# Attention of a two-stage kernel: two PSUM pairs become one ring of four, and GpSimd's and VectorE's work is put in another order

## What is computed

```python
x1 = x + tanh(g_xattn) * cross_attention(layernorm(x), ctx)          # not touched
y = layernorm(x1)
q, k = heads(y @ Wq), heads(y @ Wk)                                  # 8 heads of 64
gl_v = (y @ Ws).reshape(b, t, h, e)                                  # 5 experts
wv = topk_mask(gl_v, 2) * sigmoid(gl_v)
xv = einsum('btd,edk->btek', y, Wv)
v = einsum('bthe,btek->bhtk', wv, xv)                                # values, mixed over experts
probs = softmax(einsum('bhid,bhjd->bhij', q * scale, k))
attn = einsum('bhij,bhjd->bihd', probs, v)
mask_o = topk_mask((y @ Wd).reshape(b, t, h, e), 2)
out = einsum('bthe,bthk,ekd->btd', mask_o, attn, Wo)                 # expert results, summed over heads
return x1 + tanh(g_ffn) * out
```

## Time and profile before

| | |
|---|---|
| median of 3 runs | 1397.97 us (1397.93 to 1398.26) |
| the profiled execution, its time | 1396.65 us |
| its span in the profile | 1394.9 us |
| PE, DVE, ACT, POOL busy over the span | 90%, 63%, 46%, 53% |
| first layer / second layer | to 565 us / from 565 us to the end |

### The profile page before, as it was taken

How to read it: one execution, slowest core, us unless ns; L and a number is a source line. 1 busy time by engine, 2 the same in 40 slices (tenths; PEclk the granted TensorE clock), 3 DMA queues, 4 the chain that set the end, 5 groups by cost and what they waited for, 6 DMA issues and landing times.

```text
span 1394.9 us, 20101 instructions
## 1 busy us (share of the span) xinstructions
PE 1261.2 (90%) x6376; PEld 919.2 (66%) x6376; DVE 876.4 (63%) x1555; ACT 639.0 (46%) x1402; POOL 742.5 (53%) x531
## 2 busy tenths in 40 slices
PE   5789898998989899679999999999899899999995
PEld 4678787777878787655657566566566566575653
DVE  6767686858585846376656646654765666566443
ACT  4433333424243421446456455555545555654551
POOL 3626161616152524384494585664763963945853
PEclk9899999999999999899999999999999999999998
DMA  7131313222121213300002001001010010010010
GB/s 239 49 113 45 105 53 98 77 74 93 60 103 61 97 47 106 117 1 9 23 9 83 0 23 68 0 32 58 0 60 30 0 60 30 0 60 0 17 43 31
DMA packets 40713, 75.73 MB, mean 54 GB/s; under 512 B 3760, under 2 KB 4272, under 8 KB 40688
## 3 DMA queue, kind: packets, MB, share of 16 engines
q1 hardware_dynamic: 40688, 75.42, 15.8%
HBM read 58.63 MB, written 16.78 MB: 54 GB/s over the span
## 4 chain that ended last, share of the span: by engine, by line
PE 36%; POOL 14%; issue 5%; DVE 3%; ACT 1%; POOLq 1%; DVEq 0%; ACTq 0%
PE ps_r L1563 7%; PE ps_r L1575 6%; POOL v_acc L1157 5%; PE ps_o L1638 5%; PE ps_p L1626 5%; PE ps_s L1615 5%; PE ps_r L1598 5%; POOL spare L1151 4%; POOL z L1169 4%; POOL v_acc L1151 1%; PE ps_r L1552 1%; PE ps_r L1589 1%; DVE sig L1420 1%; DVE nmax L1334 1%; PE ps_r L1582 0%
## 5 line engine op out<-in xcount | busy, mean ns | idle before, releaser
L1334 DVE TENSOR_REDUCE nmax<-ps_s 128x1 f32<-128x512 f32 x256 | 173.9, 685 | 207.1 <-PE ps_s L1615 206.9
L1212 ACT ACTIVATE probs<-ps_s,nmax 128x512 f32<-128x512 f32 x256 | 176.3, 689 | 263.1 <-DVE nmax L1334 260.4
L1169 POOL TENSOR_TENSOR z<-z,z_tmp 128x1280 f32<-128x1280 f32 x56 | 163.6, 2922 | 156.0 <-DVE z_tmp L1348 143.4
L1157 POOL TENSOR_TENSOR v_acc<-v_acc,spare 128x512 f32<-128x512 f32 x128 | 165.6, 1293 | 10.0
L1615 PE MATMUL ps_s<-k,q 64*128 64x512 f32 x768 | 124.3, 428 | 46.2 <-ACT probs L1212 44.6
L1626 PEld LDWEIGHTS ps_p<-ident,probs 128*128 128x128 f32 x1024 | 115.5, 142 | 73.1 <-issue 52.6
L1626 PE MATMUL ps_p<-ident,probs 128*128 128x128 f32 x1024 | 160.4, 283 | 1.7 <-ACT pt L1221 1.7
L1221 ACT ACTIVATE pt<-ps_p 128x512 f32<-128x512 f32 x256 | 152.0, 594 | 3.6 <-PE ps_p L1626 3.6
L1151 POOL TENSOR_TENSOR spare<-xv,pick 128x512 f32<-128x512 f32 x128 | 136.3, 1065 | 10.0
L696 PE MATMUL ps_f<-wh,h_t 128*128 128x512 f32 x384 | 107.9, 437 | 31.2 <-DVE x_sb L639 31.2
L226 POOL TENSOR_TENSOR e_t<-e_t 128x512 fp32r<-128x512 f32 x32 | 40.3, 1295 | 179.6 <-ACT e_t L433 179.6
(11 more groups left out here) (165 smaller groups left out, 2232.5 us busy)
## 6 DMA issues: line engine op xcount, KB each, us to landing
stage<-in_x SPq DMA_DIRECT2D x32, 256.0 KB, 2.8
stage<-in_ctx SPq DMA_DIRECT2D x32, 256.0 KB, 3.1
x_sb<-in_x SPq DMA_DIRECT2D x8, 1024.0 KB, 5.1
x_dram<-x_sb SPq DMA_DIRECT2D x32, 256.0 KB, 2.0
stage<-x_dram SPq DMA_DIRECT2D x8, 1024.0 KB, 5.7
spare<-x_dram SPq DMA_DIRECT2D x8, 1024.0 KB, 5.7
out_dram<-spare SPq DMA_DIRECT2D x32, 256.0 KB, 2.0
stage<-in_ctx_t SPq DMA_DIRECT2D x28, 256.0 KB, 2.6
```

The source lines that it names most:

```text
L1157: pool.tensor_tensor(acc, acc, v_tmp[:], ALU.add).then_inc(v_steps, 1)
L1169: pool.tensor_tensor(zv, zv, z_tmp[:, h % 2], ALU.add).then_inc(z_pool, 1)
L1212: act.activation(probs[:, n % PROBS, :], ps_s[:, n % 2, :], ACT.Exp, bias=nmax[:, n:n + 1], accum_out=den[:, h, t:t + 1]).then_inc(p_exp, 1)
L1334: dve.tensor_reduce(nmax[:, n:n + 1], ps_s[:, n % 2, :], AX_X, ALU.max, negate=True).then_inc(nmax_ready, 1)
```

## The change

`ps_s` and `ps_p` become one tensor of four banks. Tile n has bank n % 4 for its scores, and the turned probabilities of the tile are written over the scores in the same bank. `scores` of step n waits for the copy (`pt_ready`) of tile n - 3 and no longer for an exponential. Both turns of a pair of tiles stand together behind the scores of the next even step; the copy on ACT has a lag of 2 steps in place of 3. The eight value products of a pair become one block (16 matmuls in the trace). POOL mixes the values of all four pairs and then sums heads 1 to 5; heads 6 and 7 are summed by DVE (`mix_sum`, waits for POOL's fifth sum and for itself, `z_ready`). The comparisons for values and for the mask become one set of eight instructions over both at step 1, with count at step 2 and routing at step 3. Nearly every table has other numbers.

```diff
-    TURN_Y_AT = [-11, -11, -10, -9]
-    EXPERTS_AT = [[-9], [-8, -7], [-5, -4], [-3]]
-    Q_AT = [[-6, -6], [1, 2], [6, 6], [18, 18]]
-    K_AT = [[-3, -2], [3, 4], [10, 10], [19, 19]]
-    PV_AT = [11, 12, 12, 13]
-    TURN_O_AT = [17, 25, 34, 41]
-    TURN_Z_AT = [45, 45, 45]
-    RESULT_AT = [[46], [47], [47, 48], [49]]
+    TURN_Y_AT = [-11, -11, -10, -10]
+    EXPERTS_AT = [[-9], [-7, -6], [-2, -1], [-1, 0]]
+    Q_AT = [[-8, -7], [1, 2], [6, 7], [16, 17]]
+    K_AT = [[-4, -3], [4, 5], [8, 9], [18, 20]]
+    PV_AT = 11
+    TURN_O_AT = [15, 21, 29, 37]
+    TURN_Z_AT = [42, 43, 43]
+    RESULT_AT = [[45], [45, 46], [46], [47]]
...
-    LO_BEHIND = {"q": 2, "k": 2, "turn_z": 0}
+    LO_BEHIND = {"turn_z": 0}
+    BANKS = 4
+    COPY_LAG = 2
...
             def scores(b, n, first):
-                if n or not first:
-                    pe.wait_ge(p_exp, b * STEPS + n)
+                if n >= BANKS or not first:
+                    pe.wait_ge(pt_ready, b * STEPS + n + 2 - BANKS)
...
-            def turn_probs(b, n, first):
+            def turn_probs(b, n):
                 pe.wait_ge(p_exp, b * STEPS + n + 1)
-                if n >= 2 or not first:
-                    pe.wait_ge(pt_ready, b * STEPS + n - 1)
...
-                if part == 1 and 0 <= n - LAG < STEPS:
-                    turn_probs(b, n - LAG, first)
+                if part == 1 and n % 2 == 0:
+                    for before in (n - 2, n - 1):
+                        if 0 <= before < STEPS:
+                            turn_probs(b, before)
...
+            def batch(b, first=False):
+                for p in range(PAIRS):
+                    mix_values(b, p, first)
+                for p in range(LAST_PAIR):
+                    mix_sums(b, p)
...
+            def mix_sum(b, h):
+                dve.wait_ge(z_dve, b * H + h + 1)
+                if h == 2 * LAST_PAIR:
+                    dve.wait_ge(z_pool, (b + 1) * POOL_SUMS)
+                else:
+                    dve.wait_ge(z_ready, b * 2 + 1)
+                zv = z[:].rearrange("p t (e k) -> p t e k", e=E)
+                dve.tensor_tensor(zv, zv, z_tmp[:, h % 2], ALU.add).then_inc(z_ready, 1)
```

More of the change, by code:

```diff
@@ L955, in expert_attention @@
         v_acc = sb("v_acc", [P, PAIRS, NT, 2, DH])
-        probs = sb("probs", [P, PROBS, T])
+        probs = sb("probs", [P, BANKS, T])
         pt = sb("pt", [P, 4, NT, T])
@@ L1207, in scores_exp @@
                 act.wait_ge(nmax_ready, b * STEPS + n + 1)
-                if n >= PROBS or not first:
-                    act.wait_ge(pt_ps, b * STEPS + n - PROBS + 1)
+                if n >= BANKS or not first:
+                    act.wait_ge(pt_ps, b * STEPS + n - BANKS + 1)
                 h, t = head_tile(n)
-                act.activation(probs[:, n % PROBS, :], ps_s[:, n % 2, :], ACT.Exp, bias=nmax[:, n:n + 1],
+                act.activation(probs[:, n % BANKS, :], ps_s[:, n % BANKS, :], ACT.Exp, bias=nmax[:, n:n + 1],
                                accum_out=den[:, h, t:t + 1]).then_inc(p_exp, 1)
@@ L1392, in part_lo, with compare, count_better @@
                                              ALU.mult, ALU.add).then_inc(out_ready, 1)
-            def compare(b, s, experts):
+            def compare(b):
                 dve.wait_ge(logits_ready, b * NT + NT)
-                groups = slice(s * NT * H, (s + 1) * NT * H)
-                for k in experts:
-                    for others, before in ((slice(k + 1, E), ALU.is_gt), (slice(0, k), ALU.is_ge)):
-                        if others.stop > others.start:
-                            dve.tensor_tensor(beaten[:, groups, k, others], logits[:, s, :, others],
-                                              logits[:, s, :, k:k + 1].broadcast_to([P, NT * H, others.stop - others.start]),
-                                              before).then_inc(compared, 1)
-            def count_better(b, s):
-                dve.wait_ge(compared, (2 * b + s + 1) * COMPARISONS)
-                dve.tensor_reduce(logits[:, s], beaten[:, s * NT * H:(s + 1) * NT * H], AX_X, ALU.add).then_inc(gates, 1)
+                both = logits[:].rearrange("p s g e -> p (s g) e")
+                square = beaten[:].rearrange("p g k j -> p g (k j)")
+                for d in range(1, E):
+                    early, late = both[:, :, 0:E - d], both[:, :, d:E]
+                    for first_place, other, than, order in ((d, late, early, ALU.is_gt), (d * E, early, late, ALU.is_ge)):
+                        places = square[:, :, bass.ds(first_place, E - d, step=E + 1)]
+                        dve.tensor_tensor(places, other, than, order).then_inc(compared, 1)
+            def count_better(b):
+                dve.wait_ge(compared, (b + 1) * COMPARISONS)
+                dve.wait_ge(sig_exp, b + 1)
+                dve.tensor_reduce(logits[:].rearrange("p s g e -> p (s g) e"), beaten[:], AX_X, ALU.add).then_inc(gates, 1)
             def count_values(b):
-                dve.wait_ge(sig_exp, b + 1)
                 dve.tensor_scalar(sig[:], sig[:], 1.0, None, ALU.add).then_inc(gates, 1)
-                count_better(b, 0)
             def route_values(b, first):
-                dve.wait_ge(gates, b * 4 + 1)
+                dve.wait_ge(gates, b * GATES + 2)
                 dve.reciprocal(sig[:], sig[:]).then_inc(gates, 1)
@@ L1449, in step @@
                 if part == 3:
-                    for half, experts in enumerate((range(0, E // 2), range(E // 2, E))):
-                        if n == GATES_AT + half:
-                            compare(b, 0, experts)
-                        if n == MASK_AT + half:
-                            compare(b, 1, experts)
-                    if n == ROUTE_AT[0]:
+                    if n == GATES_AT:
+                        compare(b)
+                    if n == GATES_AT + 1:
+                        count_better(b)
                         count_values(b)
-                    if n == ROUTE_AT[1]:
+                    if n == ROUTE_AT:
                         route_values(b, first)
-                    if n == MASK_AT + 2:
-                        count_better(b, 1)
-                    if n == MASK_AT + 3:
-                        route_out(b, first)
                     if n == NORMALISE_AT:
@@ L1646, in step @@
                     scores(b, n, first)
-                if part == 1 and 0 <= n - LAG < STEPS:
-                    turn_probs(b, n - LAG, first)
+                if part == 1 and n % 2 == 0:
+                    for before in (n - 2, n - 1):
+                        if 0 <= before < STEPS:
+                            turn_probs(b, before)
                 if part == 2:
                     for p in range(PAIRS):
-                        for k in range(NT):
-                            if n == PAIR * p + PV_AT[k]:
-                                values(b, p, k, first)
+                        if n == PAIR * p + PV_AT:
+                            values(b, p, first)
                     for what in parts_at(n):
```

88 lines of the change are left out of this document (38 added, 50 removed).

## The result

The changed kernel takes 1421.49 us (median of 4 runs, 1418.13 to 1421.99) where the kernel before takes 1398.12 (1397.93 to 1399.74) on the same chip: a ratio of 1.0159, 95% interval 1.0142 to 1.0177. It is 1.6% slower. The profiled execution, the fastest of the four, took 1418.13 us with a span of 1416.3. The time lies inside the stated range (1378 to 1425) and above the forecast's own (1394 to 1420).

The account below looks back on a forecast made before the run. PE was taken to set the second layer's 98.05 us period; terms summed to +3.0 per period, +21 us over seven, less 12 at the ends, giving 1407 us, 0.6% slower (own range 1394 to 1420, stated range 1378 to 1425).

Parts of the forecast that it names:

- so 0: Comparison set at step 1: meets an idle POOL, is done about when step 2's scores are, and costs 0 per period.
- waits removed: PE's three `scores` waits for exponentials (4.5 us) and `turn_z`'s wait for POOL (0.9) go: -5.4 us per period.
- blocks merged: On PE, joined turns, value products in one block and fewer halves save 2.9 us per period.
- third `turn_y`: PE waits there for DVE to finish h3, behind `turn_o` of pair 1 in the ring: +4.5 us per period.
- second `turn_y`: PE waits there for ACT's read of the high half of `k` of pair 3: +1.2 us per period.
- third `turn_z`: PE waits there for the low half of `k` of pair 2: +0.85 us per period.
- sums on DVE: Sums of h6 and h7 on DVE delay the scores of step 10 and turn 9: +2.4 us per period.
- clock: PE's clock drops in every period behind the 4.5 us wait: +2.1 us per period, bounds 0 and 3.
- The ends: Start and tail of the changed layer together: 12 us shorter, bounds -5 and -18.
- Rival 1: Freed slack wins: doubtful terms at their lower bounds, period 1.7 us shorter, 1374 us, faster; chance 0.35.
- Rival 2: Every new PE wait also costs clock: sums 4, clock 4 us per period, 1424 us; chance 0.11.
- Rival 3: Exponentials not freed: turns wait for them as `scores` did, 2.3 us a period returns, 1423 us; chance 0.07.

Follow-up runs that it names:

- experiment 2: The changed kernel with the comparisons back in their earlier form, 16 smaller instructions at the same place: 1402.35 us.
- experiment 1: The changed kernel with `turn_o` of pair 1 four steps later (step 25 in place of 21): 1370.41 us.
- experiment 5: The changed kernel with both `turn_o` of pair 1 at step 25 and the comparisons in their earlier form: 1351.34 us.
- experiment 3: The changed kernel with 32 transposes that nothing reads put into PE's wait ahead of the third `turn_y`: 1416.5 us.
- experiment 11: The changed kernel with later `turn_o` of pair 1, earlier comparisons, and the sums of h6 and h7 one step later on DVE: 1354.97 us.
- the best version: The changed kernel with later `turn_o` of pair 1, earlier comparisons, and ACT's read of `k` of pair 2's high half moved forward: 1344.08 us.
- experiment 4: The kernel before with only the ring of four banks, `scores` waiting for a copy, joined turns and copy lag 2: 1396.09 us.
- experiment 8: The changed kernel with ACT reading the high half of `k` of pair 3 ahead of step 21's copy and exponential: 1421.43 us.

## Why the prediction was right in sign and short in size

**The step that failed is "so 0"**, the comparison set at step 1. It looked at when the comparisons can start and that POOL is idle, and gave no row for their length. They take 5.00 us in their new form (2.70 in the earlier one, experiment 2), and the maxima behind them are late for two steps. That is two waits of 1.16 us together, and with what they shift further on 1.97 us of period at full clock (experiments 1 and 5). The paragraph on it costed the place and not the instruction, though the change made both new. The trace of before had rows for the earlier form (DVE), eight comparisons with POOL idle and eight beside POOL's values:

```profile
973.85 0.69 DVE L1404 TENSOR_TENSOR beaten<-logits 128x128 bf16<-128x128 f32 x3 [6.58 <-ACT logits L1246]
976.44 0.91 DVE L1404 TENSOR_TENSOR beaten<-logits 128x64 bf16<-128x64 f32 x5
...
983.56 2.18 DVE L1404 TENSOR_TENSOR beaten<-logits 128x128 bf16<-128x128 f32 x3
986.18 3.26 DVE L1404 TENSOR_TENSOR beaten<-logits 128x64 bf16<-128x64 f32 x5
```

They cost 1.60 and 5.44 us. So the change lowered their sum on DVE, from 7.0 to 5.0, but put all of it in one place ahead of maxima that PE needs. By these rows the earlier form would take about 3.2 there (2.70 in experiment 2); the new form had no row at all, and the forecast named none.

By the terms of the sum, per period (waits from PE's timeline, the rest from PE's busy time in the windows):

| term | forecast | measured |
|---|---|---|
| waits removed | -5.4 | -5.44, all gone |
| blocks merged | -2.9 | -2.25 (busy 92.61 to 90.36, both at clock 1.00) |
| third `turn_y` | +4.5 | +4.35 |
| second `turn_y` | +1.2 | +1.46 |
| third `turn_z` | +0.85 | +0.84 |
| sums on DVE | +2.4 | +2.08 (1.13 and 0.95) |
| clock | +2.1 | +2.18 (92.54 to 90.36); 2.2 by experiment 3 |
| comparisons | 0 | +1.16 |
| small | +0.3 | 0 |
| sum | +3.0 | +4.4 |

98.05 + 4.38 = 102.43 against 102.40 in the profile; that it closes proves no term, since waits and busy time together are the period. Nor are the terms independent: of the 1.13 at the scores of step 10, counted as the sums', 0.52 went with the form of the comparisons (experiment 2), so the sums by themselves are nearer 1.6 than 2.1 and the comparisons nearer 1.7 than 1.2. The longest wait came out as walked: scores at 958.2, h3 from 963.04 to 964.5, PE at 964.58, s + 6.3. That of turn 9 was 0.95 for 1.4, that of the scores of step 10 1.13 for 1.0; the sums took 2.10 and 1.74 us, between the two bounds. The merged blocks were priced from single joins of rows and gave 0.65 less, the second largest error; which join gave less isn't parted by any run.

**What is left of the 14.5 us** between 1407 and 1421.49: 9.5 by the terms (7 x 4.35, the growth of the period, less the forecast's 21); 3.1 since the first layer, which the change doesn't touch, ended at 571.51 in place of 568.39; about 2 since the profiled execution of before was 1.3 under its median and this one 3.4 under its own. Over the thirteen profiles of this study, all with the same first layer, its end lies between 568.3 and 574.0 us, so 3 us of any comparison of two single profiles here say nothing. The ends were right: 21.4 longer in span is 30.5 (the period's 4.35, seven times) + 3.1 - 12.2, with -12 forecast. `turn_z` in the tail waits 6.07, as "about 6 us" had it. One of the forecast's own signs of being wrong did come, a wait for `pt` that it doesn't name: the 0.81 at the scores of step 6.

**The rivals.** Rival 1 had the sign wrong because it stood on the low ends of all doubtful terms, and these came in at their middles; but its mechanism is real. What stood against it, "the wait on h3 alone returns what the exponentials gave", holds (4.35 for 4.5), with the clock behind it. That experiment 1, with the h3 wait removed, comes to 1370.4, near rival 1's 1374, is chance: rival 1 had this wait in its sum. The times of rivals 2 and 3, 1424 and 1423, are the nearest of all, for other reasons than theirs. Rival 2's rows would be sums at 4 and clock at 4, and they read 2.08 and 2.18; its sum doesn't come out of its terms either, as 3.0 + 1.6 + 1.9 is 6.5 a period and some 1431. Rival 3 didn't happen: no turn waits for an exponential except behind DVE's late queue, and those 0.35 and 0.95 us are counted above (experiment 2 takes away the first, and experiment 11, with later sums, half of the second).

**The two rules.** In each of the seven periods the clock is at 0.50 behind the 4.35 us wait, so the Trainium skill's "TensorE: Matmul & The Clock Gate", Part 1, agrees, and the bound of 0 on that term could have been dropped. On the sums, the rule of "SBUF — State Buffer", "two separate sides", agrees too: `coef` lasted 2.25 us until POOL's sum ended, and POOL's two instructions beside DVE's sums took 1.1 us longer each (1.5 in the forecast's estimate).

**What stays open.** What in the new form of the comparisons makes it dear; whether the spread of the best version's runs is made of long periods; why the clock fell behind close small waits in some periods and not in the like ones next to them (experiments 3, 4, 8); and whether the second `turn_y`'s wait would be worth shortening in a version without the long one (in experiment 1 it is nearly gone by itself).

## What to carry to other kernels

Cost an instruction that the change writes in another form by its own shape, also where it seems to have cover: count what is queued behind it until the next instruction that the critical engine needs. Where pieces share a ring of banks, look at what stands three places ahead of each and who reads it last; one piece placed four steps later, with its two products, was worth 51 us here. And a wait on TensorE is worth more than its length or less: 4.35 us cost 2.2 more by the clock, and a wait shortened by 0.85 gave nothing because every other period was then 3.4 us longer than its neighbours, so compare all periods of a loop before and after an edit, not one.

## What the runs showed of the hardware

- Comparisons of 64 to 256 elements a partition with a strided bf16 output took 5.00 us for eight on VectorE, the same comparisons in sixteen instructions with a broadcast operand 2.70, GpSimd idle beside both. Fewer and larger was slower here.
- Eight comparisons of the earlier form took 1.60 us on VectorE with GpSimd idle and 5.44 beside GpSimd's values (kernel before); in the changed kernel a sum of 1280 elements took 1.54 us in the tail, GpSimd idle, and 2.10 and 1.74 in the loop beside GpSimd's values.
- After a wait of 4.35 us TensorE's granted clock was 0.50 for some 7 us in every period of the changed kernel, and for some 3.5 in four of seven of experiment 2, with the same wait ahead of it. A wait of 2.5 us was followed by 0.50 for some 3.5 us in three of seven periods of experiment 4.
- Waits of 1.13 and 0.95 us within 2.5 us were followed by a clock of 0.50 in every other period of experiment 8 and never in the changed kernel, and the periods of one loop then alternate between 100.7 and 104.1.
- A pair of TENSOR_SCALAR on VectorE (128x512, SBUF to SBUF) took 2.69 us beside GpSimd's 512-element products and 4.59 where GpSimd's 1280-element sum began inside it.
- Filling the wait of 4.35 us with transposes kept the granted clock at 1.00 behind it in every period of experiment 3, with the same work behind, so there it was the idleness that brought the drop.
